# One instruction per chunk for product and sum, and one shared fp32 copy of the source one-hots for two weight products

## The reference

```python
dst = (3125 * uniform((100000,)) ** 2.0)     # sorted; src is uniform over the nodes
...
e = edge_attr @ We.T + be                    # layer 1
a = leaky_relu(sum((h[src] + e) * attn, axis=-1), 0.01)
...
a_in  = segment_sum(feat_in[src]  * iw[:, None], dst)     # layer 2, iw = edge_weight
a_out = segment_sum(feat_out[dst] * ow[:, None], src)     # ow = edge_weight_n2
```

## Time and profile before

| | us |
|---|---|
| median of 3 runs (4694.25 to 4701.1) | 4699.4 |
| the profiled execution | 4693.4 |
| its span | 4691.6 |
| placing loop, about | 117 to 711 |
| unit loop, about | 731 to 1749 |
| POOL's transfers | 117.7 to 1540 |
| TensorE busy over the span | 3560.4 (76%) |
| VectorE busy over the span | 2729.4 (58%) |

### The profile page before, as it was taken

How to read it: one execution, slowest core, us unless ns; L and a number is a source line. 1 busy time by engine, 2 the same in 40 slices (tenths; PEclk the granted TensorE clock), 3 DMA queues, 4 the chain that set the end, 5 groups by cost and what they waited for, 6 DMA issues and landing times. The chain is left out here.

```text
span 4691.6 us, 87142 instructions
## 1 busy us (share of the span) xinstructions
PE 3560.4 (76%) x19416; PEld 2666.4 (57%) x19417; DVE 2729.4 (58%) x7745; ACT 1686.2 (36%) x5377; POOL 1202.6 (26%) x828
## 2 busy tenths in 40 slices
PE   5555557888887767999983333589999699998978
PEld 4333335777776666888862222577888444444444
DVE  7999999999987771112237777677766300000523
ACT  1444442234444440000017776577776100000110
POOL 1888888888888100000000000000000000000000
PEclk9999999999998888999985555899999899999989
DMA  2333333567767664444445544343332153442064
GB/s 102 102 102 102 101 97 86 149 177 209 218 204 241 243 237 120 134 120 144 134 112 173 162 157 151 121 140 123 117 97 76 36 208 129 160 153 79 1 249 137
DMA packets 435571, 656.93 MB, mean 140 GB/s; under 512 B 97532, under 2 KB 291767, under 8 KB 435362
## 3 DMA queue, kind: packets, MB, share of 16 engines
q1 hardware_dynamic: 354306, 526.63, 36.2%
q10 hardware_dynamic: 53040, 121.95, 7.2%
q0 software_dynamic: 28144, 7.36, 2.5%
HBM read 438.84 MB, written 216.02 MB: 140 GB/s over the span
## 5 line engine op out<-in xcount | busy, mean ns | idle before, releaser
L989 POOL DMA_INDIRECT slots<-all_B,put_index x800 | 1179.2, 1474 | 345.7 <-issue 240.8
L1725 POOL DMA_DIRECT2D out_dram<-all_B x7 | 8.5, 1221 | 2242.2 <-DVE all_B L1709 2242.2
L965 PE MATMUL put_ps<-put_right_in,put_left_in 128*128 128x125 f32 x2380 | 351.6, 298 | 138.6 <-ACT put_left_in L835 138.2
L765 DVE TENSOR_SCALAR put_hot<-all_iota_bf,put_words_in 128x125 bf16<-128x125 bf16 x2400 | 445.3, 315 | 3.3 <-DMA put_words_in<-slots 3.3
L1220 PE MATMUL lm_ps<-lm_v,lm_node 125*128 x1220 | 170.0, 184 | 328.4 <-DVEq L1087 127.3
L1185 ACT ACTIVATE lm_raised<-lm_hot,srt_words 128x125 f32<-128x125 bf16 x1200 | 360.3, 385 | 140.2 <-DVE lm_top L1100 64.6
L965 PEld LDWEIGHTS put_ps<-put_right_in,put_left_in 128*128 128x128 f32 x2380 | 307.1, 204 | 167.8 <-ACT put_left_in L835 157.4
L835 ACT CAST put_left_in<-put_hot 128x640 f32 (+1 forms) x238 | 172.5, 725 | 629.6 <-issue 321.8
L2262 DVE TENSOR_TENSOR upd_pre<-upd_po,upd_bias 125x512 f32<-125x512 f32 x25 | 17.3, 692 | 630.5 <-PE upd_po L2193 630.5
L1835 PE MATMUL att_ps<-att_right,att_left 128*125 128x125 f32 x2380 | 318.7, 286 | 68.4 <-ACT att_right L1856 64.6
L969 PE MATMUL put_ps<-put_right_out,put_left_out 128*128 128x125 f32 x2380 | 342.7, 297 | 0.0
(11 more groups left out here) (346 smaller groups left out, 5955.9 us busy)
## 6 DMA issues: line engine op xcount, KB each, us to landing
c_T<-counts SPq DMA_DIRECT2D x255, 312.5 KB, 2.9
pair<-put_T ACTq DMA_DIRECT2D x125, 625.0 KB
hot<-put_hot SPq DMA_DIRECT2D x480, 160.0 KB
att_ring<-hot SPq DMA_DIRECT2D x240, 320.0 KB, 3.2
all_A<-in_edge_attr_dram SPq DMA_DIRECT2D x100, 448.0 KB
lm_planes<-src_rows SPq DMA_DIRECT2D x123, 320.0 KB, 3.7
counts<-put_T ACTq DMA_DIRECT2D x125, 312.5 KB
lm_hot<-hot SPq DMA_DIRECT2D x120, 320.0 KB, 3.0
```

Source lines behind the costliest of these rows:

```text
L765: ins = v.tensor_scalar(hot[:, h, t, c * S:c * S + P], k["iota_bf"][:, :], words_in[:, j, c, t:t + 1], None, ALU.is_equal)
L965: ins = t_.matmul(tile(1, c), left_in[:, c, :], right_in[:, c, :], start=False, stop=False, skip_group_check=True)
L989: nc.gpsimd.indirect_dma_start(slots, bass.IndirectOffsetOnAxis(index[:, C * g + j:C * g + j + 1], 0), stage[:, C * g + j, :], None).then_ ...
```

## The change

It has two parts. In `edge_dot` the product and the sum are replaced by eight instructions, one for each of the eight edges of a partition, which multiply 128 features with the vector and sum them at once; `multiplied` goes, and SyncE waits for `dotted`. In the unit loop one fp32 tile `wide` of the source one-hots serves both groups of products: as the left operand of the first, and, without its last columns, as the right operand of the second. The second weight is multiplied into the destination one-hots (`left_out`), in place of the plain cast; `right_out` goes. ScalarE, which writes `wide`, waits for `summed_out` where it waited for `summed_in`.

```diff
-        left_in, left_out = b.sb("left_in", [L, HALF, S]), b.sb("left_out", [L, HALF, S])
-        right_in, right_out = b.sb("right_in", [L, HALF, P]), b.sb("right_out", [L, HALF, P])
+        wide = b.sb("wide", [L, HALF, S])
+        right_in, left_out = b.sb("right_in", [L, HALF, P]), b.sb("left_out", [L, HALF, S])
...
-                        sp.wait_ge(multiplied, g - 1 + HEAD)
+                        sp.wait_ge(dotted, g - 1 + HEAD)
...
                     dve.wait_ge(loaded[h], 32 * (2 * i + u // 2) + 32)
-                    v.tensor_tensor(prod[:, h, :, :], ea[:, h, :, :], f["vrow"][:, :].unsqueeze(1).to_broadcast([P, C, DE]),
-                                    ALU.mult).then_inc(multiplied, 1)
-                    dve.wait_ge(multiplied, g + 1 + HEAD)
                     dve.wait_ge(staged, g - 3 + HEAD)
-                    v.tensor_reduce(dot[:, u, :], prod[:, h, :, :], AX.X, ALU.add).then_inc(dotted, 1)
+                    for c in range(C):
+                        ins = v.tensor_tensor_reduce(prod[:, h, c, :], ea[:, h, c, :], f["vrow"][:, :], 1.0, 0.0, ALU.mult, ALU.add,
+                                                     dot[:, u, c:c + 1])
+                    ins.then_inc(dotted, 1)
...
                         dve.wait_ge(summed_out, u + 1)
-                        v.tensor_copy(left_out[:, :, :], hot_of[:, h, DST, :, :])
-                        v.tensor_tensor(right_out[:, :, :], hot_of[:, h, SRC, :, 0:P], field(WOUT), ALU.mult).then_inc(outs, 1)
+                        v.tensor_tensor(left_out[:, :, :], hot_of[:, h, DST, :, :], words_in[:, j, :, WOUT].unsqueeze(2).to_broadcast([L, HALF, S]),
+                                        ALU.mult).then_inc(outs, 1)
...
                     act.wait_ge(hots, u + 1)
-                    act.wait_ge(summed_in, u + 1)
-                    nc.scalar.copy(left_in[:, :, :].rearrange("p c n -> p (c n)"),
+                    act.wait_ge(summed_out, u + 1)
+                    nc.scalar.copy(wide[:, :, :].rearrange("p c n -> p (c n)"),
...
-                            ins = t_.matmul(tile(1, c), left_in[:, c, :], right_in[:, c, :], start=False, stop=False, skip_group_check=True)
+                            ins = t_.matmul(tile(1, c), wide[:, c, :], right_in[:, c, :], start=False, stop=False, skip_group_check=True)
...
-                            ins = t_.matmul(tile(2, c), left_out[:, c, :], right_out[:, c, :], start=False, stop=False, skip_group_check=True)
+                            ins = t_.matmul(tile(2, c), left_out[:, c, :], wide[:, c, 0:P], start=False, stop=False, skip_group_check=True)
```

More of the change, by code:

```diff
@@ L528, in phase_front @@
         blocks_in, loaded = [b.sem(f"blocks_in{h}") for h in range(2)], [b.sem(f"loaded{h}") for h in range(2)]
-        based, cols_hot, rows_hot, multiplied, dotted, picked, placed = (
-            b.sem(n) for n in ("based", "cols_hot", "rows_hot", "multiplied", "dotted", "picked", "placed"))
+        based, cols_hot, rows_hot, dotted, picked, placed = (
+            b.sem(n) for n in ("based", "cols_hot", "rows_hot", "dotted", "picked", "placed"))
         counted, carried, negated, looked = (b.sem(n) for n in ("counted", "carried", "negated", "looked"))
@@ L677, in turn @@
                             place(chain, i, 0)
-                for sem in (rows_hot, cols_hot, multiplied, dotted, picked, placed):
+                for sem in (rows_hot, cols_hot, dotted, picked, placed):
                     dve.sem_inc(sem, HEAD)
```

## The result

The changed kernel takes 4775.9 us (median; 4772.8 to 4780.0), the kernel before 4696.8 beside it (4693.0 to 4701.1): a ratio of 1.0169 (1.0151 to 1.0186), slower by 79.0 us. The forecast was 4718 in a range of 4650 to 4780. The sign is right and the time lies near the top of the range, but the loss is four times the one forecast. The span of the profiled execution is 4771.0 us, 4691.6 before; the granted clock of TensorE over the whole is 0.891, 0.908 before.

What follows compares the result with a forecast made beforehand. VectorE was taken to bound the placing loop; in the unit loop VectorE bounds long blocks, ScalarE one-unit blocks, and both nearly tie in two-unit blocks. Terms -7, +21 and +5 made +19 us: 4718 us, range 4650 to 4780.

Steps and rivals of the forecast that it cites:

- product and sum: Placing loop: eight multiply-and-sum instructions with accumulator reads take 2.32 us a group, a gain of 0.07; -7 us in 100 groups.
- later cast, clock held: Unit loop: ScalarE's cast waits for the second group of products, lengthening blocks of two units from 7.67 to 8.2 us; +21 us.
- TensorE's clock: Unit loop: products now in the chain feel each drop to the lower clock level; 0 to +20 us, taken as +5.
- rival A: Placing loop: the sum comes without a read that takes a slot, -70 us in place of -7: 4655; chance 0.12.
- half-rate case: Placing loop: the new instructions run at half rate, a pair 0.42 us, +97 us: 4822; chance 0.06.
- rival C: Placing loop: the dot product is slower than what it replaces; full read +46 us (4771), chance 0.12, or the half-rate case.
- Rival D: POOL is locked out in the placing loop and the unit loop waits for its transfers, +20 us: 4738; chance 0.10.
- gaps at the reads: Placing loop: gaps at the accumulator reads would let POOL in earlier than now; no size given.
- long blocks: Unit loop: the five blocks of seven or eight units take 25.3 us against 26.9 and more, -8 us.
- list of signs: What in the trace would show each step right or wrong, such as two-unit blocks at 8.2 us or TensorE products doubled.
- B: VectorE bounds the unit loop throughout: 0.46 us saved in each of 238 units, -110 us: 4582; chance 0.07.
- one-unit blocks: Unit loop: blocks of one unit, where ScalarE is the limit, stay unchanged at 4.8 us.

Runs made afterwards that it cites:

- e9: The kernel before with only the first part of the change (eight multiply-and-sum instructions in place of product and sum): 4641.8 us, ratio 0.9877.
- e10: The changed kernel with 16 small TensorE products of zeros added per unit, behind the count products: 4665.8 us, ratio 0.9925.
- e11: The kernel before with the first part of the change and 16 small products of zeros per unit, old cast order: 4610.2 us, ratio 0.9811.
- e8: The changed kernel with ScalarE's cast in two pieces, so that TensorE's in-products start behind the first: 4714.3 us, ratio 1.0022.
- e12: The kernel before with one line changed: ScalarE's cast waits for summed_out, not summed_in, tiles still apart; 4814.8 us, ratio 1.0241.
- e4: The same code as e10 (changed kernel, 16 small products of zeros per unit) on another chip: 4773.2 us, ratio 1.0064.

## Why the forecast was right in sign and wrong in size

The sum by its own terms, against the runs:

```
term                        forecast   measured   from
product and sum                 -7      -55.5     e9 against before
later cast, clock held         +21      +55.6     e10 less e11
TensorE's clock                 +5      +77       below
sum                            +19      +77       (the change: +79.0)
```

The measured terms add up to the change by the way they are formed (e9, e10 and e11 cancel), so the sum checks nothing. The attention layer's 6 us are in the first two of them. Without it, at the last evacuation of the profiled executions, the terms are -46.9, +49.5 and +80.6, together +83.2.

The clock's term: the changed kernel less e10 is 2.31 per cent by the ratios, 108.6 us of 4700. Of these, 31.6 were lost with the old order too. The rest is 77.

**Product and sum: mis-sized, and rival A was true.** I charged the accumulator's read with a slot of 0.07 us, from tiny instructions of other kinds. The pair takes 0.21, as rival A had it (a pair under 0.25). The 0.69 us a group would be 69 us, but the first cast came only 49.9 us earlier in the changed kernel (735.8 to 685.9). L658 took most of the rest: 0.197 us each before, 0.554 now, 50 times, 17.9 us. It starts at 406.09 and ends at 406.71, under a transfer of POOL that runs from 405.55 to 406.74. In 44 of its 50 executions it took over 0.3 us and ended with a transfer that was under way when it started; in the kernel before one of the 50 started under a transfer. That is the price of an instruction that was costed at nothing because it was not touched. The half-rate case of rival C is dead: between L2366 (256 elements, 0.43 us) and L635 (1,024, 1.21) an element costs 1.02 ns, so at half that rate 128 elements alone would take 0.26 us, and the whole pair takes 0.21. The Trainium skill's rule ("Vector Engine (DVE) Microarchitecture Reference", section "Points that are easy to get wrong") names one form, `S2S2D2_STT`, with two sources in SBUF that are not bf16, which halves its throughput. L2366's 0.43 us disagrees with it, and carried over to the new instruction, as the forecast did for its rival, it doesn't hold either.

**POOL: the other way.** Rival D had it locked out. It got in more: a transfer took 1315 ns on average and not 1474, and the last ended at 1410.3 us and not at 1540.4.

```profile
L989 POOL DMA_INDIRECT slots<-all_B,put_index x800 | 1051.9, 1315 | 342.9 <-issue 240.1 <-ACT all_B L808 99.4 <-DMA slots<-all_B,put_index 3.4
```

The transfer at 402.45 runs through the first pairs in 1.24 us, a free one in 1.19. The 3.30 us of the earlier trace rows is gone with the long product: in the kernel before, 97 transfers that met L635 took 2.66 us on average in the placing loop; in the changed kernel 192 met the eight new instructions and took 1.25. The forecast's rule (two inputs in SBUF lock POOL out) would have covered these eight too, for they read two operands in SBUF as well. Its remark that gaps at the reads would let POOL in had the right outcome; whether it is the reads that let it in, no run shows. What the forecast left out is the other direction: POOL's transfers, now where VectorE's small instructions are, hold L658 up.

**The later cast: the mechanism was right, its numbers were taken at their best.** Casts are released by L969 where L965 stood, as forecast. For a block of n units the form "evacuation to cast, plus so much for each further unit, plus cast to evacuation" holds. With the clock held, e10's two-unit blocks give 4.35 + 3.50 + 0.74 = 8.59 us (medians of the three parts), and the same numbers give 12.09 for three units (measured 12.13), 15.59 for four (15.65) and 26.1 for seven (26.16). I had 4.05 + 3.41 + 0.76. The 3.41 was the span to the evacuation's start and not to a cast; with the later cast in one piece, two casts are never closer than 3.50 in any run. The 4.05 was the row that I happened to open: the median of the kernel before is 4.14, and of two-unit blocks in e10 4.35. Why it grew by 0.2 us is open; the trace puts it down to issue. Per block this is little. Over the 72 blocks of two or more units it makes about 30 us, an estimate from the medians above, and the loops' part of the term is 49 us against a forecast of 21. The long blocks that were to give 8 us back gave about 3, in the four that lie between two evacuations (e10 against e11).

**The clock: the step that failed.** The forecast saw that idle time between units grows, and allowed 0 to +20 us for it from the mean of one stretch (0.99 at 83% busy). That mean belongs to the old order. What the change makes is a gap of 2.3 us in the typical two-unit block, and what is behind the gap is in the chain: 1.11 us more for L965 and 0.54 for L969, 1.65 in each block that has it. At 55 two-unit blocks that alone would be 91 us. An upper bound could have been set ahead of the result, as an estimate: the 2.66 us of products in a unit (1.38 and 1.28) at twice their length in each of 55 blocks, 146 us. That the range held the time is luck: rival C, which was not what happened, had stretched it to 4780, and this bound was not in it. The list of signs did name it ("products at double length ... would make the clock's term larger than the chain's"): the mechanism was seen and had no price.

**The rivals.** A was true and was hidden under the second part. B is dead: VectorE has 182.8 of 276 us. (Its price took 0.46 us a unit, where the forecast's own saving was 0.50.) C in both forms and D are dead. The one-unit blocks did not stay unchanged: their median went from 4.95 to 5.09 us (4.82 in e10).

What stays open: why the attention layer is 6 us shorter in five of the traces; what else makes the changed kernel slower than its parts added; why POOL gets in beside the new instructions; the 0.2 us between evacuation and cast; and the stalls of the first chip.

## What to carry to other kernels

When an edit lengthens the wait of an engine whose clock can fall, price the work behind the gap at the lower level at once and put it into the range; the mean clock of the old order says nothing about the new one. Two tiles for two readers cost VectorE 0.5 us a unit that nobody waited for, and bought ScalarE a start 1.1 us earlier that everybody waited for: look at who may start when the tile comes free, before counting the instructions that sharing saves. And time a change's parts apart: here one part gained 55 us, and the other lost 2.4 per cent, some 112 us (ratio 1.0238; its wait alone 1.0225 and 1.0241). Look outside the edited loops as well: 6 us of that gain lay in a layer that nobody had touched.

## What the runs showed of the hardware

- The accumulator's read behind a custom instruction of VectorE has a record of 0.074 us and takes no slot of its own: the next instruction starts with it, start to start 0.21 us for 125x128 in fp32. Whether it is part of that 0.21, no run shows.
- TensorE's level was low behind idle gaps of 2.33 us (changed kernel), and fell during the products behind 2.13 (e8) and 1.58 (e12). It held behind one of 1.06 with 16 small products ahead of it (e10), but also behind one of 2.45 in the kernel before: the length of the last gap alone doesn't tell. Ten products took 1.38 us at the upper level and 2.49 at the lower.
- Small products of zeros in a gap are cheap: in the old order 16 per unit and 8 per unit can't be told apart (ratios 0.9811 and 0.9802, intervals overlapping), and 16 are 32 us faster than none (4610.2 and 4641.8, one group).
- A transfer of POOL can hold a small instruction of VectorE: L658, 125x16 in fp32, grew from 0.197 to 0.554 us on average and ended with the transfer. The Trainium skill ("SBUF — State Buffer", section "Who interferes with whom") says that who issues first holds the shared ports and the other waits in full, and counts tensor_scalar among the instructions that can take them. The trace agrees in part, with its 406.71 and 406.74. L659 of the kernel before, the same instruction form, started 0.09 us into a transfer (410.41 and 410.32) and took its usual 0.17. In the placing loops of the two traces none of the 99 tensor_scalar instructions of this size that started in the first 0.5 us of a transfer was held, and 49 of 51 that started between 0.5 and 0.9 us into one were.
- One code lay 1.4 per cent apart on two chips in its ratio to the kernel before (e4 1.0064, e10 0.9925), with waits of up to 7.2 us on one of them.
